# The last step's scores and outputs moved ahead of five pairs, dense chunks put between late pairs, and a landing wait at every third out

## What is computed

```python
# block 1: linear attention with MLP projections, causal, without softmax
xn = layernorm(x)
q, k, v = [gelu(xn @ W1 + b1) @ W2 + b2 for each of q, k, v]
scores = tril(q @ k.T / sqrt(256 * 512))
x = x + layernorm(scores @ v) * ln_w + ln_b
# block 2: each position s has one of 8 tiles, idx[s], by its position code
xn = layernorm(x)
x = x + (xn @ W[idx[s]].T + b[idx[s]])
```

## Time and profile before

| | |
|---|---|
| three runs, median (lowest to highest) | 316.1 us (315.4 to 316.92) |
| profiled execution, its own time | 315.08 us |
| its span, and granted TensorE clock | 313.3 us, 0.977 |
| TensorE matmuls busy | 289.5 us (92%) |
| VectorE busy | 235.7 us (75%) |
| ScalarE busy | 188.7 us (60%) |
| GpSimd busy | 176.6 us (56%) |
| chain that ended last | TensorE 73%, VectorE 11%, issue 5% |

### The profile page before, as it was taken

How to read it: one execution, slowest core, us unless ns; L and a number is a source line. 1 busy time by engine, 2 the same in 40 slices (tenths; PEclk the granted TensorE clock), 3 DMA queues, 4 the chain that set the end, 5 groups by cost and what they waited for, 6 DMA issues and landing times.

```text
span 313.3 us, 5485 instructions
## 1 busy us (share of the span) xinstructions
PE 289.5 (92%) x1806; PEld 256.9 (82%) x1806; DVE 235.7 (75%) x539; ACT 188.7 (60%) x380; POOL 176.6 (56%) x238
## 2 busy tenths in 40 slices
PE   8999999998999999999999999999998976594994
PEld 6788898986898988889788988899988965583983
DVE  5868788899879879968986896798568667272556
ACT  2646777666756876676778667678664353372400
POOL 6881633351584659475646626584565757276551
PEclk9979999999999999999999999999999999699899
DMA  7909960020011110311221000250142331832011
GB/s 221 231 0 330 354 216 1 0 69 33 6 68 67 42 64 2 94 43 39 63 73 64 9 0 20 85 167 20 70 132 78 114 131 69 256 133 80 32 42 34
DMA packets 24209, 27.83 MB, mean 89 GB/s; under 512 B 4659, under 2 KB 22068, under 8 KB 24118
## 3 DMA queue, kind: packets, MB, share of 16 engines
q1 hardware_dynamic: 15910, 13.68, 14.8%
q0 software_dynamic: 3296, 8.64, 8.0%
q10 hardware_dynamic: 4976, 5.16, 4.9%
HBM read 13.95 MB, written 14.44 MB: 91 GB/s over the span
## 4 chain that ended last, share of the span: by engine, by line
PE 73%; DVE 11%; issue 5%; ACT 4%; another core or an unknown queue 2%; POOL 2%; DMA 1%; DVEq 0%; ACTq 0%; POOLq 0%; SPq 0%
PE ring L491 41%; PE o_ps L491 9%; PE s_ps L491 6%; PE w_ps L491 2%; ACT xn L982 2%; DVE xres L1451 2%; PE ring L500 2%; PE ring L519 2%; PE sc_ps L604 2%; PE ring L761 1%; POOL out_dram L1744 1%; PE sc_ps L602 1%; DVE xres L1219 1%; DVE xnT L1147 1%
## 5 line engine op out<-in xcount | busy, mean ns | idle before, releaser
L491 PE MATMUL ring<-xnT,w_sp 128*128 128x512 f32 x288 | 74.4, 403 | 3.0 <-DVE hT L1152 1.1
L491 PEld LDWEIGHTS ring<-xnT,w_sp 128*128 128x128 f32 x288 | 52.7, 191 | 15.2 <-issue 3.3
L882 ACT ACTIVATE ring<-ring,b_cols 128x512 f32<-128x512 f32 x48 | 31.7, 660 | 28.4 <-PE ring L491 27.0
L491 PE MATMUL ring<-hT,w_sp 128*128 128x512 f32 x192 | 46.8, 398 | 0.0
L1152 DVE TENSOR_TENSOR hT<-ring,hT 128x512 fp32r<-128x512 f32 x48 | 32.5, 681 | 14.6 <-ACT hT L885 13.0
L491 PEld LDWEIGHTS ring<-hT,w_sp 128*128 128x128 f32 x192 | 35.8, 190 | 8.3 <-DVE hT L1152 0.2
L1679 POOL DMA_INDIRECT sorted_rows<-xres,slot_i x30 | 31.3, 1044 | 8.5 <-issue 6.5
L1645 POOL TENSOR_TENSOR vtok<-v,vtok 128x512 fp32r<-128x512 f32 x14 | 18.0, 1287 | 26.5 <-ACT vtok L902 26.5
L1744 POOL DMA_INDIRECT out_dram<-slot_rows x22 | 21.7, 987 | 18.4 <-DVE slot_rows L1437 13.1
L885 ACT CAST hT<-ring 128x512 fp32r<-128x512 f32 x48 | 28.2, 587 | 1.5
L1219 DVE SCALAR_TENSOR_TENSOR xres<-cen,rs,xres 128x256 f32<-128x256 f32 x32 | 23.7, 754 | 3.2 <-issue 3.2
(11 more groups left out here) (245 smaller groups left out, 680.8 us busy)
## 6 DMA issues: line engine op xcount, KB each, us to landing
sorted_rows<-blank ACTq DMA_DIRECT2D x1, 5032.0 KB, 20.8
xt<-x SPq DMA_DIRECT2D x7, 512.0 KB, 3.5
slot_rows<-sorted_rows SPq DMA_DIRECT2D x22, 136.0 KB
w_stage<-tile_w SPq DMA_DIRECT2D x8, 256.0 KB, 2.7
h<-sorted_rows SPq DMA_DIRECT2D x15, 136.0 KB
xt<-x SPq DMA_DIRECT2D x2, 256.0 KB, 3.0
hT<-position_table POOLq DMA_DIRECT2D x1, 512.0 KB, 9.2
sorted_rows<-xres,slot_i POOLq DMA_INDIRECT x30
```

Source lines behind the costliest of these rows:

```text
L491: last = te.matmul(o, lhs[k][a], rhs[k][c], start=start and k == 0 and i == 0, stop=stop and k == n - 1 and i == 2, skip_group_check=check)
L882: nc.scalar.activation(full, ring[(2 + m) % 3][:, :], ACT.Gelu, bias=b1c[:, m // 2, m % 2:m % 2 + 1]).then_inc(gelu, 1)
```

## The change

- TensorE makes the last step's scores and first outputs ahead of the products of pair 4 and the transposes of pair 5, and outputs 2 and 3 ahead of the transposes of pair 6; ScalarE's and VectorE's lists follow. Pairs 6 to 9 come after that, each with its transposes and products in a row.
- The dense chunks take position 12 of the transposes (`place`, `LATER = 12`), in a buffer of their own (`kT`). A dense product goes before the products of each of pairs 12 to 17, the last two behind pair 17. They write `o_ps`; pairs from 8 on write three banks in turn instead of five.
- VectorE aggregates and centres the last step's outputs two at a time.
- GpSimd scatters the second half of step 6 only when the last step's first two outputs are made (`o_ready`), and has outs 9 to 12 between the parts of the last step.
- From out 6 on, every out with a number divisible by three waits until all outs since out 4 have landed.

```diff
-AMID, INNER, MIDDLE = 1, 5, 8
+AMID, INNER, MIDDLE, LATER = 1, 5, 8, 12
...
+        def place(m):
+
+            return m if m < LATER else LATER if m == PAIRS else m + 1
...
+            return w_ps if m < MIDDLE else [ring[2], w_ps, s_ps][(m - MIDDLE) % 3]
...
+            if m == PAIRS:
+                return kT[:, 0].rearrange("p k n -> p (k n)")[:, a * GT:a * GT + GT]
...
-                te.wait_ge(xb_lo, AMID + PAIRS + 1)
-                if i < Y_BANKS:
-                    te.wait_ge(y_done, AMID + PAIRS + i - Y_BANKS + 1)
+                if i == 0:
+                    te.wait_ge(xb_lo, AMID + LATER + 1)
+                if i < 2:
+                    te.wait_ge(o_cen, CH * STEPS)
                 else:
-                    te.wait_ge(dense_done, 2 * (i - Y_BANKS + 1))
-                mm3(pair_y(PAIRS + i)[:, :], [[pair_xb(PAIRS, a)[:, cols(2 * e + k)] for a in range(2)] for k in range(KC)],
+                    te.wait_ge(dense_done, 2 * (i - 1))
+                mm3(o_ps[i % 2][:, :], [[pair_xb(PAIRS, a)[:, cols(2 * e + k)] for a in range(2)] for k in range(KC)],
...
+                elif m == MIDDLE + 2:
+                    te.wait_ge(o_cen, CH * LAST + 3)
                 else:
-                    te.wait_ge(y_done, AMID + m - Y_BANKS + 1)
+                    te.wait_ge(y_done, AMID + m - 2)
...
-            pair_products(4)
             last_scores(0)
-            pair_transposes(5)
             last_scores(2)
             last_scores(3)
             last_state(0)
             last_state(1)
-            pair_products(5)
-            pair_transposes(6)
+            pair_products(4)
+            pair_transposes(5)
             last_out(0)
             last_out(1)
             last_state(2)
+            last_out(2)
+            pair_products(5)
+            last_state(3)
+            last_out(3)
+            pair_transposes(6)
             pair_products(6)
             pair_transposes(7)
-            last_out(2)
             pair_products(7)
             pair_transposes(8)
-            last_state(3)
-            last_out(3)
+            pair_products(8)
             pair_transposes(9)
-            for m in range(MIDDLE, PAIRS):
-                if m + 2 <= PAIRS:
-                    pair_transposes(m + 2)
+            pair_products(9)
+            pair_transposes(10)
+            pair_transposes(11)
+            pair_products(10)
+            pair_transposes(12)
+            pair_products(11)
+            for m in range(LATER, PAIRS):
+                pair_transposes(m + 1)
+                dense_products((m - LATER) // 4, (m - LATER) % 4)
                 pair_products(m)
-            for e in range(DENSE):
-                for g in range(NT // 2):
-                    dense_products(e, g)
+            for i in range(PAIRS - LATER, NT):
+                dense_products(i // 4, i % 4)
...
             def pair_norm(m):
-                slot_norm(AMID + 2 * m)
-                slot_norm(AMID + 2 * m + 1)
+                p = place(m)
+                if p >= 2:
+                    act.wait_ge(xb_t, AMID + p - 1)
+                elif p == 1:
+                    act.wait_ge(xb_t, AMID)
+                for h in range(2):
+                    row_norm(AMID + 2 * m + h, AMID + 2 * p + h)
 
             def pair_rounded(m):
-                act.wait_ge(xb_t, AMID + m + 1)
+                p = place(m)
...
-            pair_norm(5)
-
             last_rounded(1)
             last_rounded(0)
+            pair_norm(5)
+            last_rounded(2)
+            scores_rounded(LAST)
             pair_rounded(5)
-            last_rounded(2)
             pair_norm(6)
-            scores_rounded(LAST)
             pair_rounded(6)
             pair_norm(7)
             pair_rounded(7)
             pair_norm(8)
             pair_rounded(8)
             pair_norm(9)
-            for m in range(MIDDLE + 1, PAIRS + 1):
+            pair_rounded(9)
+            pair_norm(10)
+            pair_rounded(10)
+            pair_norm(11)
+            pair_rounded(11)
+            pair_norm(PAIRS)
+            pair_rounded(PAIRS)
+            for m in range(LATER, PAIRS):
+                pair_norm(m)
                 pair_rounded(m)
...
+            def last_aggregates(cs):
+                dve.wait_ge(o_stat, cs[-1] + 1)
                 alone(dve, gate_dve)
-                nc.vector.bn_aggr(mv2[:, c, :], st2[:, c, :]).then_inc(o_aggr, 1)
-                dve.wait_ge(o_aggr, c + 1)
-                nc.vector.scalar_tensor_tensor(out=cen[:, c, :], in0=o, scalar=mv2[:, c, 0:1], in1=lnw_row[:, :],
...
-            pair_out(4)
             last_masked(0)
             last_v_rest(1)
             last_rest(0)
-            pair_rest(5)
             last_masked(2)
             last_masked(3)
             last_rest(2)
             scores_rest(LAST)
-            pair_out(5)
-            pair_rest(6)
+            pair_out(4)
+            pair_rest(5)
             out_centred(LAST, 0)
             out_centred(LAST, 1)
-            pair_out(6)
-            pair_rest(7)
+            last_aggregates((0, 1))
+            last_centred((0, 1))
+            out_centred(LAST, 2)
             x1_final(LAST, (0, 1))
             x1_stats(LAST, (0, 1))
             x1_var(LAST, (0, 1))
-            out_centred(LAST, 2)
+            pair_out(5)
+            pair_rest(6)
+            out_centred(LAST, 3)
+            last_aggregates((2, 3))
+            last_centred((2, 3))
+            pair_out(6)
+            pair_rest(7)
+            x1_final(LAST, (2, 3))
+            x1_stats(LAST, (2, 3))
+            x1_var(LAST, (2, 3))
             pair_out(7)
             pair_rest(8)
-            out_centred(LAST, 3)
+            pair_out(8)
             pair_rest(9)
-            x1_final(LAST, (2, 3))
-            pair_out(8)
-            x1_stats(LAST, (2, 3))
+            pair_out(9)
             pair_rest(10)
-            x1_var(LAST, (2, 3))
-            pair_out(9)
             pair_rest(11)
-            for m in range(MIDDLE + 2, PAIRS):
-                if m + 2 <= PAIRS:
-                    pair_rest(m + 2)
+            pair_out(10)
+            pair_rest(PAIRS)
+            pair_out(11)
+            for m in range(LATER, PAIRS):
+                pair_rest(m)
+                g = m - LATER
+                dense_out(g // 4, g % 4 * 2)
+                dense_out(g // 4, g % 4 * 2 + 1)
                 pair_out(m)
-            for e in range(DENSE):
-                for t in range(NT):
-                    dense_out(e, t)
+            for g in range(PAIRS - LATER, NT):
+                dense_out(g // 4, g % 4 * 2)
+                dense_out(g // 4, g % 4 * 2 + 1)
...
-                    pool.wait_ge(o_aggr, cs[-1] + 1)
+                    pool.wait_ge(o_aggr, cs[0] // 2 + 1)
...
                     pool.wait_ge(y_done, n + 1 if n < AMID else AMID + (n - AMID) // 2 + 1)
+                    if n > REUSED and n % 3 == 0:
+                        pool.wait_ge(sent[1], 16 * (n - REUSED))
...
-            rows_sorted(s, range(CH))
-
-            slots((7, 8, 9, 10, 11, 12))
+            rows_sorted(s, (0, 1))
+            slots((7, 8))
+            pool.wait_ge(o_ready, CH * LAST + 2)
+            rows_sorted(s, (2, 3))
             rstd_out(LAST, (0, 1))
-            slots((13, 14))
+            slots((9, 10))
             rstd_x1(LAST, (0, 1))
             rows_sorted(LAST, (0, 1))
-            slots((15, 16))
             rstd_out(LAST, (2, 3))
-            slots((17, 18))
+            slots((11, 12))
             rstd_x1(LAST, (2, 3))
-            slots(range(19, SLOTS))
+            slots(range(13, SLOTS))
```

More of the change, by code:

```diff
@@ L745, in slot_products, with pair_transposes @@
                     [[wf[:, a, k, bass.ds(tiles[n], C)] for a in range(2)] for k in range(KC)]).then_inc(y_ps, 1)
-            def pair_transposes(m):
-                te.wait_ge(xnb_done, AMID + 2 * m + 2)
-                if m == INNER:
+            def pair_transposes(p):
+                te.wait_ge(xnb_done, AMID + 2 * p + 2)
+                if p == INNER:
                     te.wait_ge(v_sum, 2 * STEPS)
-                elif m < MIDDLE:
-                    te.wait_ge(xb_lo, AMID + m)
-                elif m == MIDDLE:
+                elif p < MIDDLE:
+                    te.wait_ge(xb_lo, AMID + p)
+                elif p == MIDDLE:
                     te.wait_ge(off_lo, 3)
                     te.wait_ge(diagonal, CH - 1)
-                elif m == MIDDLE + 2:
+                elif p == MIDDLE + 2:
                     te.wait_ge(xb_lo, AMID + MIDDLE)
-                elif m > MIDDLE + 2:
-                    te.wait_ge(xb_lo, AMID + m - 2)
+                elif p > MIDDLE + 2:
+                    te.wait_ge(xb_lo, AMID + p - 2)
                 for i in range(4):
-                    last = te.transpose(pair_t(m)[:, cols(i)], xn[:, (AMID + 2 * m + i // 2) % CH, cols(i % 2)], ident[:, :])
```

(28 more changed lines are left out.)

32 lines of the change are left out of this document (11 added, 21 removed).

## The result

The changed kernel took 323.93 us (median of 4 runs, 323.62 to 324.32), the kernel before on the same chip 316.22: the ratio is 1.0242, 95% interval 1.0218 to 1.0267. It is slower, as forecast, but by 7.7 us and not 2.8, and the time lies above the range. The profiled execution took 323.94 us, its span is 322.2, against the 316.1 of the sum.

A forecast was written before the change was run, and what follows sets the result against it. GpSimd's outs, each third waiting for landings, were to set the end: out 13 at 268.9, out 36 at 313.5 after corrections, span 316.1 against 313.3, +2.8 on the median 316.1 makes 318.9 us, 0.9% slower; range 314.5 to 322.5.

The forecast's parts named there:

- The failed step: End of the kernel: out 36 starts at 313.5, lands by 315.7, and the span ends 0.4 us later, at 316.1.
- The rival with cheap landings: GpSimd's outs: undisturbed and faster landings, or a 0.3 us restart, leave the time within 0.5%; chance 0.20.
- The head: GpSimd between 246 and 269 us: serial scatters, outs and last-step parts put out 13 at 268.9, before at 258.30.
- Landings beside the loads: Outs 11 and 14 land among 16 loads: 1.1 us added, between bounds of 0 and 2.5.
- the late slots: Late outs hold few real rows: 1.5 us taken off for quicker landings of four groups, bounds 0 and 3.
- The price of a wait: Every third out on GpSimd: 3.22 us from start to start instead of 1.28, so 1.94 us each.
- The one near 250: TensorE's signal seen by the masks at 250.06, 2.3 us after their scores ended; expected not to recur.
- four or more: Number of back-to-back indirect DMAs on GpSimd, one per 1.28 us, behind which TensorE's signals were read as coming late.
- The rival that three are already too many: TensorE's signals stay late behind bursts of three; 14 us of slack cover it, sum unchanged; shares 0.55 with the forecast.
- The signal into the serial head: Rival: TensorE's outputs reach GpSimd late behind four DMAs, delaying everything after; span 318.4, 321.2 on the median; chance 0.12.
- TensorE's branch: Pairs and dense products: six rounds of 3.19 us to 295.9, branch ends at 302.2, 14 us ahead of GpSimd's.
- The second rival: Throttle hidden, TensorE's branch sets the end; with waits of w us, 302 + 8w, faster under about 1.2; chance 0.13.

The follow-up runs named there:

- e3: The kernel before with waits for landing at outs 34, 35 and 36 only: 320.39 us, ratio 1.0137.
- e5: The kernel before with GpSimd held back at the end of its list until the dense chunk's store has landed: 321.95 us, ratio 1.0177.
- e10: The changed kernel, but every third out, from out 9, waits for the landing of the out before the one before it: 311.74 us, ratio 0.9894.
- e2: The kernel before with only the change's landing waits at every third out added: 324.41 us, ratio 1.0276.
- e1: The changed kernel without its landing waits at every third out: 314.48 us, ratio 0.9960.
- e4: The changed kernel with step 6's scatter in one piece again, not held for the last step's outputs, landing waits kept: 324.37 us, ratio 1.0284.
- e12: The kernel before with only a wait at every third out for the landing of the out before the one before it: 311.67 us, ratio 0.9896.
- e6: The changed kernel with landing waits at outs 15, 18 and 21 alone: 318.99 us, ratio 1.0093.

## Why the prediction was wrong

**The failed step is the last one of the sum**: "Out 36 then starts at 313.5 and lands by 315.7", and from the landing 0.4 us to the end, 316.1. I took the distance from the store's landing to the span's end for the program's whole end, because in the kernel before SyncE's wait was last. But the end moved to another engine, and the last engine's own end goes with it: GpSimd leaves 5.63 us after its last indirect DMA (e3 and e5 show it apart from the rest). From the start of out 36 to the span's end it is 6.84 us, not 2.6. That is 4.2 of the 6.1 us by which the span was missed. The rival with cheap landings fails by the same step.

**The other 1.9 us** are the start of out 36, 315.36 instead of 313.5, and come from several terms. The whole profiled execution ran 1.05 us late before the change begins: step 5's first scatter starts at 218.27, before at 217.22. The head was 1.6 us shorter than summed: the scatter behind the outputs started 0.27 us after them and not 0.79, and most of the steps taken from the earlier trace rows came out 0.2 to 0.5 us shorter, since the idle times inside them were shorter or gone (power and shift with their gaps 1.32, from 257.65 to 258.97, where I had 1.77). Landings beside the loads cost 1.1 us at out 12 and 1.5 at out 15, together 2.6 where I had put 1.1, and just above my upper bound of 2.5: I argued that the loads would be half done, and they were not. And the late slots gave back less: 39.85 us for seven threes against 39.0, since landings of nearly empty slots save 0.3 us in a wait, not more. 1.05 - 1.6 + 1.5 + 0.9 is 1.9.

**The price of a wait was right**: 1.94 us in the sum; a full three took 5.82 us (275.51 to 281.33), which makes 1.98, and the last one 5.48, which makes 1.64. By "DMA: Bandwidth & Descriptors" of the Trainium skill, section "Anatomy of one DMA", an estimated 1.8 came out, between them. Its rule in "Rules for kernel authors", to wait on a DMA's semaphore late, is the one that these runs bear out: e10 differs from the changed kernel in waiting for an older landing and in starting at out 9, and its ratio is 0.9894 where that of the change is 1.0242.

**What else the text named.** After 262 us TensorE's signals are no longer late, as forecast, but not because of the new order: e2 has none there either, and e1, with the new order and no waits, has one of 4.1 us. The one near 250 is another matter: it stays in e2 and is gone in e1, where the new order has two scatters and not four ahead of outs 7 and 8; but it is gone in e4 too, which has six in a row, and in e12, which has the old order, so no run says what removed it. The one near 224 stays. Late signals belong to long series of indirect DMAs, as I read from the earlier trace rows, but "four or more" was too low: four gave none that a timeline shows, five gave one in every trace, six gave one in the kernel before and e3 but none near 250 in e4 and e12, and eight or ten always did. The rival that three are already too many falls too.

The signal into the serial head did not come: GpSimd's scatter went out 0.27 us after TensorE's outputs had ended (251.34). TensorE's branch ended later than summed, its dense products at 303.3: the rounds took 3.6 us instead of 3.19, most of it since a pair's products start 1.73 us after the dense product ahead of them (282.51 to 284.24) and not 1.40. It cost nothing under GpSimd's tail.

The second rival, a throttle with cheap waits, is what e10 makes of the change; its formula, 302 + 8w, gives 307.6 at 0.7 us each, and 310.6 was measured, 3.0 more. The failed step puts 4.2 on top (6.8 us from the start of out 36 to the end, not 2.6), and 1.2 go off, since out 36 started at 303.81 and the formula has it at 305.0; the formula counts 24 gaps of 1.28 us between 24 outs, one too many.

**Where the expected gain went.** e1 shows the new order by itself: 0.4%. VectorE's branch is 4 us shorter there (307.1 against 311.2), and the drain, 0.7 us below the old end, takes over at 312.6. The kernel before was 0.7 us from being bound by it, so the waits, which move GpSimd's last out by 9.4 us from e1 (305.99) to the change (315.36), went straight into the time.

## What to carry to other kernels

Before you sum a change that moves the end from one engine to another, read every engine's last instructions and how far each lies under the end; an engine's own exit is part of its branch. If one engine's long series of indirect DMAs makes others stand for nothing the profile can name, a short pause every few was enough here (e10, e12): wait for a landing that is already due, not for the one just issued. And a pause is free only while the engine has slack; if it falls behind its work, the series afterwards can be longer than the one that was broken up (ten outs in e6, eight in e1).

## What the runs showed of the hardware that was not expected

- GpSimd's final drain ends 5.63 us after the end of its last indirect DMA in the thirteen traces where it follows at once, and takes the same 5.62 us when GpSimd has stood idle for seven us before it (e5). Whether a program without indirect DMAs has it too was not tried.
- A row scatter landed 2.1 to 2.4 us after its start by itself, and about 3.5 us (out 11) and 3.9 us (out 14) beside the loads; these two are worked out from the starts of outs 12 and 15, less the 0.84 us from a landing to the next start in the changed kernel's chain of waits (303.35 to 304.19).
- ScalarE or VectorE can stand for 4 to 7 us for a TensorE signal during a series of eight to ten indirect DMAs, for 3.1 us behind six (the kernel before), and for 1.2 to 1.4 us behind five (near 224 us, all traces). No timeline shows it behind series of up to four, with a pause of 0.7 us between them in e10, where the out ahead of the pause was still under way. What holds the signal up is not settled: the traces show only when it is seen.
